# A convolution layer and a recurrent layer on one core: one conv tap of the smaller channel group moved to ScalarE and GpSimd, and one step of the recurrence split into three single-pass products

## The reference

```python
# layer 0 (inner = 192, hidden = 384)
p = layernorm(x) @ w_in + b_in
local = depthwise_conv_3x3(p, k_conv)                    # 9 taps per channel
mixed = 0.25 * (four directional EMA scans of local) + local
x = x + (layernorm(mixed) @ w_out + b_out)
x = x + (gelu(layernorm(x) @ w1 + b1) @ w2 + b2)
# layer 1
xn = layernorm(x)
u, g = xn @ Wu + bu, sigmoid(xn @ Wg + bg)
h = 0
for _ in range(8):
    h = g * (h @ A) + (1 - g) * u
x = x + h
x = x + (gelu_tanh(layernorm(x) @ mlp_w1 + b1) @ mlp_w2 + b2)
```

## Time and profile before

| | us |
|---|---|
| median of 3 runs | 230.45 (229.41 to 230.69) |
| the profiled execution's own time | 230.32 |
| its span | 228.4 |
| busy in the span: PE | 219.6 (96%) |
| PEld | 182.3 (80%) |
| DVE | 182.7 (80%) |
| ACT | 137.0 (60%) |
| POOL | 148.8 (65%) |
| granted TensorE clock | full speed in all 40 slices |

### The profile page before, as it was taken

The page is one execution under the profiler, slowest core; times in us unless marked ns, Lnnn a source line. Parts: engine busy times, 40 slices in busy tenths (PEclk is TensorE's granted clock), DMA queues, the critical chain, the costliest instruction groups (busy, mean ns, idle before and its releaser), DMA issues.

```text
span 228.4 us, 4138 instructions
## 1 busy us (share of the span) xinstructions
PE 219.6 (96%) x1332; PEld 182.3 (80%) x1332; DVE 182.7 (80%) x463; ACT 137.0 (60%) x308; POOL 148.8 (65%) x179
## 2 busy tenths in 40 slices
PE   8988896999999999999999999999999999999995
PEld 5676774889897989787888588888888878888885
DVE  7789999999999998996267987879696958667641
ACT  5765876768788675766563386636456552625262
POOL 7461877778979877949677573665849292836330
PEclk9999999999999999999999999999999999999999
DMA  3751000000000000000000003030313123021011
GB/s 110 214 178 54 1 0 0 4 0 0 3 0 1 3 1 0 3 0 0 0 3 0 1 36 106 34 105 0 117 58 118 56 83 93 34 70 37 0 40 63
DMA packets 11972, 9.30 MB, mean 41 GB/s; under 512 B 1232, under 2 KB 11696, under 8 KB 11952
## 3 DMA queue, kind: packets, MB, share of 16 engines
q1 hardware_dynamic: 11664, 8.97, 12.7%
q10 hardware_dynamic: 288, 0.09, 0.2%
HBM read 5.31 MB, written 3.74 MB: 40 GB/s over the span
## 4 chain that ended last, share of the span: by engine, by line
PE 80%; DVE 9%; DMA 4%; POOL 3%; issue 2%; SPq 1%; ACT 1%; DVEq 0%; POOLq 0%
PE bank L1410 12%; PE pA L1410 9%; PE pM L1361 8%; PE pM L1705 8%; PE bank L1535 7%; DMA x_all<-in_x 4%; DVE cA L1076 3%; PE bank L1578 2%; PE bank L1477 2%; PE bank L1583 2%; PE pA L1448 2%; PE bank L1680 2%; PE bank L1679 2%; PE bank L1685 2%; PE bank L1460 2%
## 5 line engine op out<-in xcount | busy, mean ns | idle before, releaser
L427 POOL TENSOR_TENSOR rs<-var,power 128x4 f32<-128x4 f32 x32 | 32.4, 1012 | 21.3 <-DVE var L967 18.2
L1076 DVE SCALAR_TENSOR_TENSOR cA<-pA,cols,cA 128x528 f32<-128x528 f32 x54 | 40.7, 754 | 0.2
L1361 PEld LDWEIGHTS pM<-w,hid 128*128 128x128 f32 x192 | 28.4, 191 | 5.7 <-issue 1.0
L1705 PEld LDWEIGHTS pM<-w,hid 128*128 128x128 f32 x168 | 26.9, 190 | 4.5
L1156 DVE SCALAR_TENSOR_TENSOR q<-th,bank 96x256 f32<-96x256 f32 x48 | 19.2, 412 | 13.3 <-PE bank L1410 13.3
L1361 PE MATMUL pM<-w,hid 128*128 128x96 f32 x192 | 28.9, 266 | 0.0
L1410 PE MATMUL pA<-q,a_half 96*96 96x256 f32 x96 | 27.0, 380 | 0.2 <-DVE q L1156 0.2
L1076 DVE SCALAR_TENSOR_TENSOR cB<-bank,cols,cB 128x256 f32<-128x256 f32 x56 | 26.4, 471 | 0.0
L1705 PE MATMUL pM<-w,hid 128*128 128x96 f32 x168 | 25.9, 266 | 0.0
L560 POOL TENSOR_TENSOR xl<-xt,xh 96x512 fp32r<-96x512 f32 x11 | 14.2, 1292 | 17.5 <-ACT xh L897 17.5
L1535 PE MATMUL bank<-local,mix 128*128 128x384 f32 x64 | 24.8, 497 | 0.1
(11 more groups left out here) (252 smaller groups left out, 612.7 us busy)
## 6 DMA issues: line engine op xcount, KB each, us to landing
moved<-blocks SPq DMA_DIRECT2D x11, 192.0 KB, 1.9
xt<-moved SPq DMA_DIRECT2D x33, 64.0 KB, 2.0
x_all<-in_x SPq DMA_DIRECT2D x8, 192.0 KB, 2.9
out<-y SPq DMA_DIRECT2D x7, 192.0 KB, 2.1
w<-in_w SPq DMA_DIRECT2D x1, 480.0 KB, 6.5
w<-in_w SPq DMA_DIRECT2D x1, 336.0 KB, 3.3
mix<-in_mix SPq DMA_DIRECT2D x1, 256.0 KB, 3.3
out<-y SPq DMA_DIRECT2D x2, 96.0 KB, 1.6
```

What stands on the lines that cost most here:

```text
L427: pool.tensor_tensor(rs[:, :], var[:, :], power[:, :], ALU.pow).then_inc(step, 1)
L1076: dve.scalar_tensor_tensor(out=acc, in0=src, scalar=col(f"k{'AB'[grp]}{k}"), in1=acc, op0=ALU.mult, op1=ALU.add).then_inc(s["conv_step"], 1)
L1361: last = pe.matmul(psum[:, k * D:(k + 1) * D], hid[:, j * TILE + k * P:j * TILE + (k + 1) * P], wc0("w2", j * D, (j + 1) * D), start=(j == ...
L1705: last = pe.matmul(dst, hid1[:, j * TILE + k * P:j * TILE + (k + 1) * P], wc1("m2", j * D, (j + 1) * D), start=j == 0 and (k == 0 if whole ...
```

## The change

Two edits are made together.

*Layer 0.* For tiles 1 to 7, tap 8 of group B leaves VectorE. ScalarE multiplies the shifted input of group B by the tap's weight into a new tile `tap8` (128 x 256), right behind its tap 0. GpSimd adds `tap8` into cB (128 x 256, both in SBUF), between rs and xn of layernorm 2 and ahead of every later tap of cB. VectorE's tap 1 of B now waits for that sum, so the order at the start of the stage changes from 1A, 1B, var, 2A, 2B to 1A, 2A, var, 1B, 2B.

*Layer 1.* For tiles 1 to 7, step 5 of the recurrence is split: ScalarE copies the two halves of q into `q_high` (float32r), GpSimd subtracts to make `q_low`, and TensorE runs three float32r passes for each half in place of one float32 product. a_half is split once, in the turn. On GpSimd the row addition that makes x4b moves from behind `add_q(c, 3)` to the head of the stage, and x4b gets a third buffer; on ScalarE the copies stand behind the third gelu and ahead of `evac_gu`.

```diff
@@ conv_count @@
-            return k if c == 0 else 16 * c - 8 + 2 * k - 1 + grp
+            order = {(1, 0): 1, (2, 0): 2, (1, 1): 3, (2, 1): 4, (8, 0): 15, (8, 1): 14}
+            return k if c == 0 else 15 * c - 7 + order.get((k, grp), 2 * k - 1 + grp)
@@ GpSimd, body0 @@
                     inverse_std(rs2, var2, s["ln2_step"])
+                if tile_known(f) and not peeled(f, 0):
+                    pool.wait_ge(s["tap0_done"], 2 * f + 2)
+                    pool.wait_ge(s["tap8_made"], f)
+                    pool.tensor_tensor(cB[f % 2][:, :], cB[f % 2][:, :], tap8[:, :], ALU.add).then_inc(s["tap8_added"], 1)
...
@@ GpSimd, layer 1 @@
+            def split_q_low(c):
+                if tile_known(c):
+                    for h in range(2):
+                        pool.wait_ge(s["q_high_ready"], 2 * (c - 1) + h + 1)
+                        pool.wait_ge(s["q_ready"], QS * c + 2 * SPLIT_STEP + h - 1)
+                        pool.tensor_tensor(q_low[0:D, half(h)], moved(c, SPLIT_STEP)[0:D, half(h)],
+                                           q_high[0:D, half(h)].bitcast(F32), ALU.subtract).then_inc(s["q_low_ready"], 1)
...
+                if tile_known(m) and not is_last(m):
+                    add_rows4(m)
...
                 add_q(c, 1)
+                split_q_low(c)
                 add_q(c, 3)
-                if tile_known(m):
-
-                    wait(pool, s["y_ready"], m - 1)
-                    pool.wait_ge(s["x4_ready"], x4_count(m))
-                    if is_last(m):
-                        pool.wait_ge(s["xn4_ready"], 4 * m + 4)
-                    add_row(x4b[m % 2][:, :], x4[:, :], rows[:, 2 * D:3 * D], s["x4b_ready"])
+                if is_last(m):
+                    pool.wait_ge(s["xn4_ready"], 4 * m + 4)
+                    add_rows4(m)
@@ ScalarE @@
                     act.activation(acc, src, ACT.Copy, scale=col(("kA0", "kB0")[grp]))\
                        .then_inc(s["tap0_done"], 1)
+                    if grp == 1:
+                        wait(act, s["tap8_added"], f - 1)
+                        act.activation(tap8[:, :].rearrange("c (r w) -> c r w", w=SIDE), tap_views(f, 8)[1][1], ACT.Copy,
+                                       scale=col("kB8")).then_inc(s["tap8_made"], 1)
...
+            def split_q_high(c):
+                if tile_known(c):
+                    for h in range(2):
+                        act.wait_ge(s["q_ready"], QS * c + 2 * SPLIT_STEP + h - 1)
+                        if c > 1:
+                            act.wait_ge(s["step_done"], HALF_STEPS * (c - 1) + 2 * SPLIT_STEP + h + 1)
+                        act.activation(q_high[0:D, half(h)], moved(c, SPLIT_STEP)[0:D, half(h)], ACT.Copy)\
+                           .then_inc(s["q_high_ready"], 1)
...
                 gelu(2)
+                split_q_high(c)
                 evac_gu(f)
@@ VectorE, body0 @@
                             dve.wait_ge(s["tap0_done"], 2 * c + 1 + grp)
+                            if grp == 1:
+                                dve.wait_ge(s["tap8_added"], c)
...
-                    ln1_stats(lambda grp: tap(1, [grp]))
+                    ln1_stats(lambda at: tap(1 + at, [0]))
                 else:
-                    tap(1)
-                tap(2)
+                    tap(1, [0])
+                    tap(2, [0])
+                if peeled(c, 0):
+                    tap(2)
+                else:
+                    tap(1, [1])
+                    tap(2, [1])
                 tap(3)
...
-                    tap(8)
+                    tap(8, [0])
@@ TensorE, layer 1 @@
+            def split_step(c, h):
+                if tile_known(c):
...
+                    dst = step_bank(SPLIT_STEP, h)
+                    pe.wait_ge(s["q_high_ready"], 2 * (c - 1) + h + 1)
+                    pe.matmul(dst, a_high[0:D, :], q_high[0:D, half(h)], start=True, stop=False, skip_group_check=True)
+                    pe.matmul(dst, a_low[0:D, :], q_high[0:D, half(h)], start=False, stop=False, skip_group_check=True)
+                    pe.wait_ge(s["q_low_ready"], 2 * (c - 1) + h + 1)
+                    pe.matmul(dst, a_high[0:D, :], q_low[0:D, half(h)], start=False, stop=True, skip_group_check=True)\
+                      .then_inc(s["step_done"], 1)
...
                 for h in range(2):
-                    rec_step(c, 5, [h])
+                    split_step(c, h)
                     m2(g, 4 + h)
```

More of the change, by code:

```diff
@@ L73 @@
 V_BESIDE = 3
+SPLIT_STEP = 5
 REC_BANK = (4, 2, 5, 3)
@@ L186, in build @@
         cB = [sb(f"cB{k}", TOKENS) for k in range(2)]
+        tap8 = sb("tap8", TOKENS)
         local = sb("local", 2 * 2 * INNER)
@@ L195, in build @@
         q_one, q_three = sb("q_one", TILE), sb("q_three", TILE)
+        a_high, a_low = sb("a_high", D, F32R), sb("a_low", D, F32R)
+        q_high, q_low = sb("q_high", TILE, F32R), sb("q_low", TILE, F32R)
         h8 = sb("h8", TILE)
         x4, y = sb("x4", CHUNKS * D), sb("y", CHUNKS * D)
-        x4b = [sb(f"x4b{k}", CHUNKS * D) for k in range(2)]
+        x4b = [sb(f"x4b{k}", CHUNKS * D) for k in range(3)]
         blocks3, blocks4 = sb("blocks3", CHUNKS * D), sb("blocks4", CHUNKS * D)
@@ L583, in turn, with add_rows4 @@
                 ln3_std(3)
+                pool.wait_ge(s["a_high_ready"], 1)
+                pool.tensor_tensor(a_low[0:D, :], a_half[0:D, :], a_high[0:D, :].bitcast(F32), ALU.subtract)\
+                    .then_inc(s["a_low_ready"], 1)
+            def add_rows4(m):
+                wait(pool, s["y_ready"], m - 2)
+                pool.wait_ge(s["x4_ready"], x4_count(m))
+                add_row(x4b[m % 3][:, :], x4[:, :], rows[:, 2 * D:3 * D], s["x4b_ready"])
             def body1(i):
@@ L905, in turn @@
                 normalize3(2)
+                act.activation(a_high[0:D, :], a_half[0:D, :], ACT.Copy).then_inc(s["a_high_ready"], 1)
             def body1(i):
@@ L1191, in store_sum @@
                 dve.wait_ge(s["m2_done"], p + 1)
-                dve.tensor_tensor(y[:, :], bank[at][:, 0:384], x4b[p % 2][:, :], ALU.add).then_inc(s["y_ready"], 1)
+                dve.tensor_tensor(y[:, :], bank[at][:, 0:384], x4b[p % 3][:, :], ALU.add).then_inc(s["y_ready"], 1)
             def body1(i):
@@ L1237, in body1 @@
                             dve.tensor_tensor(y[:, chunks(h)], bank[(V_BANK, 7)[h]][:, 0:2 * D],
-                                              x4b[g % 2][:, chunks(h)], ALU.add).then_inc(s["y_ready"], 1)
+                                              x4b[g % 3][:, chunks(h)], ALU.add).then_inc(s["y_ready"], 1)
                     else:
@@ L1371, in ln3_transposes @@
                     if peeled(f, 0):
-                        pe.wait_ge(s["conv_step"], conv_count(TILES - 1, 8, 1))
+                        pe.wait_ge(s["conv_step"], conv_count(TILES - 1, 8, 0))
                     elif peeled(f, 1):
@@ L1412, in rec_step @@
                           .then_inc(s["step_done"], 1)
+            def split_step(c, h):
+                if tile_known(c):
+                    if c == 1:
+                        pe.wait_ge(s["a_high_ready"], 1)
+                        pe.wait_ge(s["a_low_ready"], 1)
+                    dst = step_bank(SPLIT_STEP, h)
[5 more added lines that the diff above has]
+                      .then_inc(s["step_done"], 1)
             passes = ((wi_h, xh1), (wi_l, xh1), (wi_h, xl1))
```

6 lines of the change are left out of this document (3 added, 3 removed).

## The result

The changed kernel took 231.86 us (median of 20 runs, 230.36 to 234.25), the kernel before 229.59 us (20 runs beside them, 229.03 to 230.75). The ratio is 1.0081, 95% interval [1.0061, 1.0100]: about 1.9 us slower (the two medians lie 2.3 us apart; the text goes by the ratio). The forecast was 230.9 us. The time lies in the range, but the slowing is four times the predicted 0.45 us, so a part of the cause is missing from the prediction.

What follows compares the result with a forecast made beforehand. TensorE was taken to bound layer 1, and TensorE with VectorE right beside it layer 0. Layer 0's +0.75 and layer 1's -0.25 us gave +0.5 on 230.32, with 0.13 for the median 230.9 us; range 229.4 to 232.2.

Steps and rivals of the forecast that it cites:

- Up to 0.1 us more: Layer 0: GpSimd's addition delays xn and rs by 0.5 us, and `mixed` reaches VectorE up to 0.1 us late.
- What the dropped tap gives: Layer 0: VectorE loses 2.7 us of instructions ahead of x2, which waits for TensorE; saving zero.
- The second rival: VectorE is the real bound of layer 0, so the freed tap pays; ends at 228.2 us; chance 0.06.
- What the order costs: Layer 0: direct tap pairs delay tap 8 of A, which TensorE pays in stages 2, 4 and 7; +0.75 us.
- s = 0.30: Layer 0: tap 8 of A comes 0.30 us later in each stage, bounds 0 to 0.5.
- has slack: Layer 0, stage 6: no layernorm 1 statistics there, so the later tap 8 of A adds no delay.
- It fits with 0.05 us to spare: Layer 0: GpSimd's addition into cB ends at 69.64, before VectorE asks for it at 69.69.
- the signs that the prediction named: Layer 0: idle marks for cA in stages 2 and 4, none in 3 and 6; stage 2 to 6 longer by 0.30 us.
- The first rival: The new order costs nothing and tile 1 gets through; 229.8 us; chance 0.20.
- Tiles 2 to 6 of the split: Layer 1: three-pass halves of step 5 save 0.16 us a tile, -0.80 us in five tiles.
- the third rival: GpSimd becomes late for hs in every tile of layer 1; about 233 us; chance 0.16.
- Tile 1: Layer 1: copies behind a table load make the q_three addition hold up hs; +0.60 us, bounds -0.1 to +0.9.

Runs made afterwards that it cites:

- l0_warm: Layer 0 edit alone, plus four unused TensorE products of ones in stage 2's wait for `mixed`, against the kernel before: 230.55 us, ratio 1.0022.
- after_warm: The whole changed kernel plus the four unused products of ones in stage 2's wait, against the kernel before: 230.34 us, ratio 1.0032.
- after_mended: The changed kernel plus the products of ones, with step 5 split in tiles 2 to 6 only, against the kernel before: 230.76 us, ratio 1.0047.
- l0_order_only: The kernel before with only the new order of the taps, all taps staying on VectorE: 230.68 us, ratio 1.0034.
- l1_only: Layer 1 edit alone (step 5 split for tiles 1 to 7), layer 0 as in the kernel before: 230.50 us, ratio 1.0020.
- l1_tiles2to6: Layer 1 edit alone with the split in tiles 2 to 6 only, against the kernel before: 229.19 us, ratio 0.9961.
- l1_swap17: Layer 1 edit alone, with GpSimd's q_three addition ahead of the low parts in tiles 1 and 7, against the kernel before: 229.58 us, ratio 0.9973.
- l0_tap_left_out: The kernel before, old order, with tap 8 of group B left out for tiles 1 to 7 and not replaced: 229.57 us, ratio 0.9997.
- before_pool_late: The kernel before with one unused GpSimd addition of 128x256 ahead of xn in stage 1: 230.31 us, ratio 1.0015.
- l0_only: Layer 0 edit alone (tap 8 of B moved, new order of the taps), layer 1 as in the kernel before: 231.24 us, ratio 1.0048.
- before_pool_later: The kernel before with two unused GpSimd additions of 128x256 ahead of xn in stage 1: 231.12 us, ratio 1.0058.
- after_again: The changed kernel, unaltered, run once more in a later session against the kernel before: 232.13 us, ratio 1.0089.
- the first profile: The profiled execution of the unaltered changed kernel among its first 20 runs, its slowest: 234.25 us.
- the second execution: Another profiled execution of the unaltered changed kernel, in a later session: 231.34 us.

## Why the prediction was right or wrong

**The waits for `mixed` and TensorE's clock: missed, and the largest term.** The step that failed is "GpSimd's addition ... moves xn and the next rs by 0.5 us, then ScalarE's normalization and `mixed` behind it ... Up to 0.1 us more". The delay was right in size (0.6 us). But I followed it for VectorE, in the steady stage, and not for TensorE in stage 2, where TensorE already waited for `mixed`; and I did not look at whose bank tap 8 of B sets free. These waits and their runs belong together (wait for `mixed` in stage 2 by the profile; runs with mean clock 0.993):

| kernel | wait, us | runs at 0.993 |
|---|---|---|
| l0_warm, after_warm, after_mended | 0.38 to 0.40 | 0 of 36 |
| l0_order_only, l1_only, l1_tiles2to6, l1_swap17 | 1.04 to 1.09 | 0 of 48 |
| before, l0_tap_left_out, before_pool_late | 1.53 to 1.62 | 0 of 121 |
| the change, first and second session | 2.08, 2.12 | 17 of 26 |
| l0_only | 2.13 | 9 of 12 (one at 0.991) |
| before_pool_later | 2.21 | 5 of 12 |

The waits are of one profile each, and they move with the start-up: the kernel before, whose profile has no wait for group B's bank in stage 1, shows 1.53 us, and l1_only, with the same layer 0 and such a wait, 1.09. The run of the kernel before with 0.978 is not counted.

Filling the wait takes the fall away (l0_warm, after_warm), and lengthening it in the old kernel brings it (before_pool_later): that is shown. Where in a run the fall lies is seen in three profiles only: behind the wait in after_again and l0_only (0.4 and 0.7 us after TensorE began again), ahead of it in the first profile. Not explained is the fall at 20.9 us in the first profile, since the kernel before has the same wait ahead of that place (1.51 us) and kept its clock. Nor is it shown why some runs with a 2.1 us wait keep it, or what brought the 0.978 of the one run of the kernel before.

**What the dropped tap gives: right.** Zero predicted; 0.9997 [0.9981, 1.0013] without the tap. The second rival, VectorE as the bound, falls, though VectorE was 98% busy.

**What the order costs: right in size, but in the whole edit one payment has another cause.** s = 0.30 was predicted, 0.32 stands in the rows. For the order alone +0.75 us was predicted and 1.0034 measured (+0.8 us, from 0.3 to 1.3), and it pays in stage 4, as predicted: the distances that end at the products of stages 3 to 6 are 12.39, 12.81, 12.49 and 12.36 us in l0_order_only, against 12.40 or 12.41 before. The whole edit with the clock kept measured 1.0022 (+0.5 us, from 0 to 1.0), with 12.35, 12.71, 12.39 and 12.69 us in l0_warm. So it pays in stage 6 as well, where the prediction had written "has slack", because the first layernorm's statistics are missing there. For the same reason VectorE comes to tap 1 of B sooner in that stage, and GpSimd's addition is late. "It fits with 0.05 us to spare" had been worked out for the steady stage only. VectorE and then GpSimd in stage 6 of the first profile:

```profile
84.65 1.00 DVE L1117 SCALAR_TENSOR_TENSOR cB<-bank,cols,cB 128x256 f32<-128x256 f32 x2 [0.58 <-POOL cB L554]
```

```profile
83.81 0.73 POOL L554 TENSOR_TENSOR cB<-cB,tap 128x256 f32<-128x256 f32 x1
```

The wait is 0.58 or 0.59 us in after_again, l0_warm and after_warm too. Tap 1 to tap 3 of A takes 85.57 - 82.52 = 3.05 us there, and 82.41 - 80.03 = 2.38 in l0_order_only, which has no such addition. No run moves the addition in that stage alone. Two of the signs that the prediction named came out otherwise: stages 4 and 6 have no idle mark for cA in front of the first product into pA, it only starts later; and from that product of stage 2 to that of stage 6 it is 92.72 - 42.49 = 50.23 us against 49.63 before, 0.60 longer and not 0.30.

The first rival falls: the same taps in another order, all on VectorE, are slower by 0.11 to 0.57%. The Trainium skill ("VectorE: DVE Perf Modes", "The DRAIN you can't avoid") says that a semaphore after each of eight copies cost nothing extra; for these chains through one accumulator that doesn't hold. The same section says that a next operation that is not held starts earlier, which the "never" of the prediction leaves out. A direct pair of cA took 1.61 us in all, a pace of 0.85 us, where I had 0.80.

**Tiles 2 to 6 of the split: right for four.** 0.16 us each predicted, 0.16 to 0.17 measured in tiles 3 to 6 (l1_tiles2to6 lost it again in tile 4, behind a late transfer). The third pass never waited there and hs didn't either, so the third rival falls.

**Tile 1: right in size, in part by luck.** +0.60 predicted, 13.87 - 13.17 = +0.70 measured. hs was held by the q_three addition as predicted, but that moved tile 1's stage by 0.21 us only (13.87 against 13.66 in l1_swap17), where I had made it the whole cost. 0.19 us came with a_low at the turn, which I had not seen, and the rest, 0.3 us, with the third passes: from step 5's first product to step 6's it is 140.97 - 139.41 = 1.56 us in the second execution, against 139.89 - 138.64 = 1.25 before.

**Tiles 2 and 7: missed.** In tile 2 I stopped at hs. The addition that ran late also pushed rs and xl, and xl then stood across h: +0.53 us instead of -0.16. In the second execution xl started behind h, since the transfer that it needs had landed later, and tile 2 took 12.16 us. So this term comes and goes: two of the four profiles with the split in tile 1 and the addition behind it have it (the first, l1_only), two have not (after_again, after_warm). In tile 7 -0.05 was predicted and +0.33 measured: xl, again behind the late q_three addition, held h (second execution, VectorE and then GpSimd):

```profile
215.04 1.03 DVE L1217 TENSOR_TENSOR h<-hs,q 96x256 f32<-96x256 f32 x2
```

```profile
214.19 1.27 POOL L429 TENSOR_TENSOR xl<-xt,xh 96x512 fp32r<-96x512 f32 x1
```

l1_swap17, where the addition is early, has tile 7 at 10.63 us. Layer 1 as a whole: -0.25 us predicted, +0.5 us measured (from 0 to 1.0 by the interval).

**The sum.** Predicted +0.5 us on 230.45. Measured parts: layer 0 with the clock kept +0.5, layer 1 +0.5, together near after_warm's +0.7 and near what the change itself shows in its nine runs with the clock kept (230.70 - 229.59 = +1.1). The fall, 1.6 us in 17 of 26 runs of the change, makes the rest. That the time lay inside the stated 229.4 to 232.2 us is in part luck: these bounds stood around 230.45, the median of three runs of the kernel before, and twenty runs beside the change gave 229.59. As a difference the upper bound was +1.75 us, and 1.9 was measured.
